# Second mixture of experts: three engines take two tiles in one body, with all turnings of a body in one piece

## The reference, cut to what matters

```python
logits = jnp.einsum('th,eh->te', x, router_weight)
gate = jax.nn.softmax(logits, axis=-1)
top_probs, top_idx = jax.lax.top_k(gate, TOP_K)
h_mid = jax.nn.gelu(jnp.einsum('th,ehf->etf', x, moe_w1))
expert_out = jnp.einsum('etf,efh->eth', h_mid, moe_w2)
e_ids = jnp.arange(NUM_EXPERTS)[:, None, None]
weights = jnp.sum(jnp.where(top_idx[None] == e_ids, top_probs[None], 0.0), axis=-1)
moe_out = jnp.einsum('eth,et->th', expert_out, weights).reshape(S, B, H)
return hidden_after_attn + moe_out
```

## Time and profile before

| | |
|---|---|
| median of 3 runs | 1021.64 us (1018.97 to 1023.74) |
| the profiled execution | 1022.95 us, span of its instructions 1021.2 us |
| second mixture, first turning of rows to last scatter-add | 874.28 to 1016.99 us |
| TensorE busy in the whole span | 906.8 us (89%) |
| granted TensorE clock, mean of the span | 0.938 of 2.4 GHz |

### The profile page before, as it was taken

The page is one execution under the profiler, slowest core; times in us unless marked ns, Lnnn a source line. Parts: engine busy times, 40 slices in busy tenths (PEclk is TensorE's granted clock), DMA queues, the critical chain, the costliest instruction groups (busy, mean ns, idle before and its releaser), DMA issues. The chain is left out here.

```text
span 1021.2 us, 22434 instructions
## 1 busy us (share of the span) xinstructions
PE 906.8 (89%) x6180; PEld 805.9 (79%) x6180; DVE 801.2 (78%) x2324; ACT 731.2 (72%) x1651; POOL 605.9 (59%) x699
## 2 busy tenths in 40 slices
PE   7899999999999999999999848879966751799997
PEld 5579989999999999998989736669945551599996
DVE  7589999999999999999989798757657786244443
ACT  2378889899899999999989747326654741566663
POOL 2298878877777676765555354660265278145444
PEclk8999999999999999999999968999978875799999
DMA  9276666777666666676666140347762624254453
GB/s 309 55 204 192 191 181 189 194 198 201 184 196 189 191 190 189 191 213 168 212 178 194 46 154 16 117 151 227 240 207 63 238 91 153 75 81 74 76 84 48
DMA packets 111427, 162.14 MB, mean 159 GB/s; under 512 B 16201, under 2 KB 85193, under 8 KB 110282
## 3 DMA queue, kind: packets, MB, share of 16 engines
q1 hardware_dynamic: 100200, 140.56, 46.3%
q0 software_dynamic: 10224, 18.00, 8.3%
q10 hardware_dynamic: 882, 2.14, 0.7%
HBM read 110.31 MB, written 25.17 MB: 133 GB/s over the span
## 5 line engine op out<-in xcount | busy, mean ns | idle before, releaser
L2380 POOL TENSOR_SCALAR probs<-probs,inv_sum 128x1024 f32<-128x1024 f32 (+3 forms) x128 | 303.2, 2368 | 6.7 <-DVE inv_sum L2547 6.7
L2526 DVE TENSOR_TENSOR pT_lo<-t_ps,pT_hi 128x512 fp32r<-128x512 f32 (+1 forms) x320 | 198.3, 634 | 9.1 <-ACT pT_hi L2410 7.0
L2438 ACT ACTIVATE probs<-probs,neg_max 128x1025 f32<-128x1025 f32 (+7 forms) x256 | 196.8, 771 | 5.3 <-DVE neg_max L2501 5.3
L2410 ACT ACTIVATE pT_hi<-t_ps 128x512 fp32r<-128x512 f32 (+1 forms) x320 | 172.7, 551 | 31.5 <-PE t_ps L2617 18.0
L2501 DVE CUSTOM_DVE_ANT_0 probs<-s_ps,bias_set,neg_null 128x512 f32<-128x512 f32 (+3 forms) x256 | 160.6, 645 | 2.2 <-PE s_ps L2582 2.0
L2617 PE MATMUL t_ps<-ident,probs 128*128 128x128 f32 x1152 | 157.6, 273 | 0.2 <-POOL probs L2380 0.2
L2617 PEld LDWEIGHTS t_ps<-ident,probs 128*128 128x128 f32 x1152 | 136.8, 141 | 24.1 <-issue 2.3
L2632 PE MATMUL o_ps<-pT_hi,values 128*128 128x256 f32 x576 | 148.4, 287 | 1.0 <-DVE pT_lo L2526 1.0
L2581 PE MATMUL s_ps<-k_hi,q_hilo 128*128 128x512 f32 (+3 forms) x384 | 144.7, 380 | 4.1 <-DVE q_lo L2517 1.5
L2633 PE MATMUL o_ps<-pT_lo,values 128*128 128x256 f32 x576 | 145.6, 281 | 0.0
L2582 PE MATMUL s_ps<-k_lo,q_one 128*128 128x512 f32 (+3 forms) x384 | 133.7, 348 | 0.0
(11 more groups left out here) (385 smaller groups left out, 2155.8 us busy)
## 6 DMA issues: line engine op xcount, KB each, us to landing
bias_set<-bias_dram SPq DMA_DIRECT2D x16, 1024.0 KB, 5.4
bias_set<-bias_dram SPq DMA_DIRECT2D x16, 896.0 KB, 5.3
bias_set<-bias_dram SPq DMA_DIRECT2D x16, 768.0 KB, 4.9
bias_set<-bias_dram SPq DMA_DIRECT2D x16, 640.0 KB, 4.5
q_hilo<-q_hi SPq DMA_DIRECT2D x128, 64.0 KB, 2.0
q_hilo<-q_lo SPq DMA_DIRECT2D x128, 64.0 KB, 2.0
q_one<-q_hi SPq DMA_DIRECT2D x128, 64.0 KB, 2.1
bias_set<-bias_dram SPq DMA_DIRECT2D x16, 512.0 KB, 5.5
```

Source lines behind the costliest of these rows:

```text
L2380: pool.tensor_scalar(keys, keys, inv_sum[:, x.set, 0, h:h + 1], None, ALU.mult).then_inc(normed, 1)
L2410: act.activation(pT_hi[n % 3][:, 0:count, :], t_ps[n % 3][:, 0:2 * P * count], ACT.Copy).then_inc(hi_out, 1)
L2438: act.activation(p, p, ACT.Exp, scale=-1.0, bias=neg_max[:, x.set, row.unit, h:h + 1], accum_out=row_sum[:, x.set, row.unit, h:h + 1]).the ...
L2526: dve.tensor_tensor(pT_lo[n % 3][:, 0:count, :], t_ps[n % 3][:, 0:2 * P * count].rearrange("p (n q) -> p n q", n=count), pT_hi[n % 3][:, 0 ...
```

## The change

TensorE, ScalarE and VectorE now take the tiles i and i+1 in one turn of the loop, for even i (39 tiles make 20 turns, the last with tile 38 alone). TensorE first does all turnings of the turn, those of the hidden values of i and i+1 and those of the rows of i+4 and i+5, then `up` of i+2 and i+3, then `down` of i and i+1. ScalarE and VectorE follow that order. Ahead of the loop, tile 3's rows are turned and its features made before `up(1)` and `hidden(1)`. SyncE, POOL, the buffers and the semaphores stay as they are.

```diff
--- before.py
+++ after.py
@@ -2023,12 +2023,15 @@
             features(1)
             hidden(0)
             features(2)
+            features(3)
             hidden(1)
-            high(0)
-            for i in range(ROUTED):
-                features(i + 3)
+            for i in range(0, ROUTED, 2):
+                high(i)
+                high(i + 1)
+                features(i + 4)
                 hidden(i + 2)
-                high(i + 1)
+                features(i + 5)
+                hidden(i + 3)
 
         @block.vector
         def _(dve):
@@ -2049,13 +2052,22 @@
             low(0)
             low(1)
             low(2)
-            hidden_low(0)
-            for i in range(ROUTED):
-                low(i + 3)
-                hidden_low(i + 1)
+            low(3)
+
+            def scale(i):
+                if i >= ROUTED:
+                    return
                 wait(dve, added[i % 2], 16 * ((i - BUFS) // 2 + 1))
                 dve.wait_ge(down_ready, i + 1)
                 dve.tensor_scalar(y[i % BUFS], o_ps[i % 2][:, 0:D], rows[i % BUFS][:, bass.ds(of(i) + D, 1)], None, ALU.mult).then_inc(scaled, 1)
+
+            for i in range(0, ROUTED, 2):
+                hidden_low(i)
+                hidden_low(i + 1)
+                low(i + 4)
+                scale(i)
+                low(i + 5)
+                scale(i + 1)
 
         @block.tensor
         def _(pe):
@@ -2109,13 +2123,17 @@
             turn_rows(1)
             up(0)
             turn_rows(2)
+            turn_rows(3)
             up(1)
-            turn_hidden(0)
-            for i in range(ROUTED):
-                turn_rows(i + 3)
+            for i in range(0, ROUTED, 2):
+                turn_hidden(i)
+                turn_hidden(i + 1)
+                turn_rows(i + 4)
+                turn_rows(i + 5)
                 up(i + 2)
-                turn_hidden(i + 1)
+                up(i + 3)
                 down(i)
+                down(i + 1)
```

## The result

The change made the kernel slower: median 1040.45 us (1036.03 to 1043.21, 4 runs) against 1022.69 for the kernel before in the same comparison, ratio 1.018 with a 95% interval of 1.015 to 1.021. That is 17.8 us more (15.4 to 21.7 by the interval); 1034 was forecast, 12 more. The profiled execution took 1043.21 us (span 1041.4), the one of before 1022.95.

What follows compares the result with a forecast made beforehand. TensorE was taken as the bound, busy 25.00 of every 25 us. Terms 1.25 + 3.4 + 3.1 + 3.0 + 0 + 1.7 = 12.45 us took 1022.95 to 1035.4, median 1034; 8-in-10 range 1026 to 1042.

Steps and rivals of the forecast that it cites:

- TensorE's work, passages: TensorE in the second mixture: same instructions, and passages from transposes to products cost nothing, so 0 us.
- start, wait for gelu(1): Start of the stage: features(3) ahead of hidden(1) on ScalarE makes TensorE wait 1.25 us, bounds 0.9 to 1.4.
- tiles 9 and 29, late rows and restart: Row turnings of tiles 9 and 29: held scatters make their rows late, TensorE waits 3.4 and 3.1 us.
- short waits: Odd tiles' row turnings: rows late by 0.4, 0.5 us with restart, every second body, six times, 3.0 us.
- end: Last body: down(38) waits for high and low, +1.2, while POOL's last scatter waits less, -1.1; taken as 0.
- clock: Behind a long wait TensorE runs 3.4 us at 1.2 GHz; one fall taken, 1.7 us, bounds 0 and 3.4.
- Both long waits drop the clock and the short ones are bigger: Rival: two clock falls, and short waits grow because two scatters in flight slow each other; 18.3 us, 1040, chance 0.15.
- Only the long waits: Rival: odd rows come in time and the clock stays, leaving start and two long waits; 1029 us, chance 0.18.
- No change: Rival: the hold at tile 21 is none and tile 9's wait is mostly met; 1025 us, chance 0.10.
- Transposes let the clock fall: Rival: twelve transposes in one piece run at half clock, 26 us more, 1047 to 1060 us, chance 0.02.

Runs made afterwards that it cites:

- one_piece_one_tile: Kernel before, still one tile a turn, with the hidden turning of i+1 moved ahead of the turning of rows i+3; 1023.41 us against 1022.20, ratio 1.001.
- twelve buffers: Changed kernel with 12 row buffers in the second mixture instead of 8, nothing else; 1025.20 us against 1022.20 for the kernel before, ratio 1.004.
- shifted pairs: Changed kernel with tile 0 alone ahead of the loop, then bodies of tiles 1 and 2, 3 and 4; 1050.56 us against 1024.54, ratio 1.026.
- the body of 10.20: Tile 9's body in the changed kernel with 5 unused products ahead of turn_rows of tiles 9 and 29; 1038.20 us against 1022.24, ratio 1.015.

## Why the prediction was right, and where its sizes were off

The terms, each in the order of the forecast, against the 16.4 us of the stage (without the upstream shift):

| term | forecast | measured |
|---|---|---|
| TensorE's work, passages | 0 | 0: bodies of 6.90 to 6.96 |
| start, wait for gelu(1) | 1.25 | 1.05 |
| tiles 9 and 29, late rows and restart | 3.4 + 3.1 | 3.4 + 3.0 |
| short waits | 3.0 in six bodies | 4.8 in eight bodies |
| end | 0 | 1.1 |
| clock | 1.7, one fall | 3.0, two falls |
| sum | 12.45 | 16.4 |

- **The bound and the passages.** Right, and tested alone: 0.89 us for six transposes and a product, no gain in one_piece_one_tile or with twelve buffers.
- **The start.** The wait stands where it was put, before the second hidden turning, and is 0.2 shorter, because ScalarE's instructions overlap by about 0.1 us each. The timeline of TensorE of the kernel after:

```profile
887.16 0.66 PE L2106 MATMUL m_h_ps<-ident,m_h 128*128 128x128 f32 x4 [0.78 <-ACT m_h L2013]
```

- **The long waits.** Right in place, mechanism and size: tile 9 was 3.16 us late, tile 29 2.74 (982.49 against 978.65 + 1.10), each with 0.27 to restart. Tile 20's and 21's scatters of the kernel after show the hold behind the second:

```profile
971.45 1.56 POOL L1989 DMA_INDIRECT out_dram<-yacc,xs  x1 [3.71 <-DVE yacc L2062]
976.08 1.56 POOL L1989 DMA_INDIRECT out_dram<-yacc,xs  x1 [3.08 <-DMA out_dram<-yacc,xs]
```

  They start 4.63 apart; the earlier trace rows had 4.61. The shifted pairs are the test: the holds fell on other second tiles, and the long waits went there.
- **The short waits.** The chain was right in the main: the scatters of one body start 1.86 apart, the load follows its scatter by 3.97 in the median (4.1 forecast), and the rows that were late landed 2.1 to 2.2 behind the load (tile 29's 2.4). What failed is "it falls on every second body": eight bodies are longer, by 1.02, 0.66, 0.87, 0.49, 0.20, 0.67, 0.49 and 0.44 us, 4.8 in all (two more by under 0.1). Seven of them hold a wait for rows; the one that is longer by 0.20 (963.92) shows no wait, and what it lost there is open. I had argued that a body with a wait gives the next its slack back. It does where the next is free, as behind 919.31 (927.26 to 934.16 is 6.90), but the bodies at 934.16 and 941.75 (7.59 and 7.80) stand in a row. For the second of these the trace has a reason: the chain is not equally long each time. Tile 19's load started 5.00 us behind the scatter that it waits for (POOL's timeline and SyncE's queue of the kernel after):

```profile
936.44 1.56 POOL L1989 DMA_INDIRECT out_dram<-yacc,xs  x1 [0.30 <-issue]
```

```profile
941.44 0.33 SPq L1970 DMA_DIRECT2D xs<-routed_rows  x1
```

  With 3.95 its rows would have been in time by 0.3 us. Tile 27's was 4.28. Why single scatters land late is open; one took 5.00 in the kernel before too, where nothing waited for it. And 0.1 us to restart was too little: 0.27.
- **The end.** The term was set at 0 by letting a loss on TensorE (+1.2) and a gain on POOL (-1.1) cancel. The loss came (1.4), of the gain only 0.3. TensorE's timeline of the kernel after, then POOL's:

```profile
1030.89 0.60 PE L2106 MATMUL m_h_ps<-ident,m_h 128*128 128x128 f32 x4
1033.09 0.38 PE L2117 MATMUL m_o_ps<-w_hi,m_h_hi 128*128 x1 [1.60 <-DVE m_h_lo L2048]
```

```profile
1037.24 1.56 POOL L1989 DMA_INDIRECT out_dram<-yacc,xs  x1 [1.29 <-DMA out_dram<-yacc,xs]
```

  The last scatter starts 1.6 us behind its scaling (1035.14 + 0.48), where 1.9 was before and 0.8 was forecast: it was still waiting for an earlier one to land, since POOL's scatters before it had themselves been held up (tile 36's, at 1032.53, came 2.05 behind its scaling, 0.90 before). With twelve buffers it does start 0.80 behind its scaling (1018.60 + 0.48 to 1019.88), so the gain is real where POOL isn't late. The whole is 1.1 us, inside the bounds that were given.
- **The clock.** Right in kind, one fall short: both waits of the size in the earlier trace rows were followed by 3.4 us at 0.50. Each cost 1.4 to 1.6 us and not 1.7.
- **The rivals.** "Both long waits drop the clock and the short ones are bigger", put at 1040 with a chance of 0.15, is nearest to what happened: 18.3 us by its sum, 16.4 measured. The sum of the forecast, 1034, was low; its range held because it reached over this rival, and nothing had been worked out from rows that chose one fall of the clock over two. The rival's reason for the short waits, two scatters that slow each other, is not what the trace shows in the main: scatter to load has a median of 3.97 us against 4.10 in the kernel before, and 5.00 at most in both. The loads land in 2.4 us in the median against 2.1, but those of the late tiles in 2.1 to 2.2, tile 29's apart. "Only the long waits" falls with the seven short ones. "No change" falls with the 4.63 at tile 21. "Transposes let the clock fall" falls with twelve buffers, where twelve transposes stand in one piece and the clock reads 1.00 in all stretches of 25 us from 900 on.

## What to carry to other kernels

When an order is rewritten so that something is asked for earlier, count for each ring of buffers the time from the last use of a buffer to the next need of it and set it against the measured chain (here down, scatter, landing, load, landing: 8 us, where a single scatter's landing can add 1), for the worst member of a group and not the mean: the second tile of a pair carries the issue of the first, and any hold that falls on it. Price a wait on the bounding engine by the length of the loop body that holds it, not by the idle time in the bracket, and add the slow clock behind every long one. A term that is zero because a loss and a gain cancel should be looked at twice: the gain is worth something only if its engine was not held by something else.

## What the runs showed of the hardware that was not expected

- TensorE pays for a wait beyond its idle time: 0.27 us from the turning to its second product above the count, in the body at 919.31 and again, within 0.01 us, in the body of 10.20.
- In these records the clock reads 1.00 in a hole and falls behind it, and the length of a single hole does not decide alone: in the kernel with the odd turning behind an up, holes of 2.0 and 2.4 us left the clock at 1.00; in the shifted pairs one of 2.2 us was followed by 0.50. What else counts no run here tells. The stretch of the shifted pairs behind the hole of 2.2 us (columns as above):

```profile
943.00:946.40 3.40, 3.40 (x9) 2.66 (x10) 0.15 (x1) 0.60 (x2) 0.11 (x1) 0.50 0.49 80
```

- A plain float32 product of 256 columns takes 0.43 us and stands in the profile as two records.
